# Two graph layers on one core: first loads in blocks, paired first projections, leading matmuls, adjacency waits by quarter

## The reference

```python
deg = sum(adj, -1)
agg = (adj @ x) / maximum(deg, 1e-6)
h = layernorm(x + relu(concat([x, agg], 2) @ W.T))
Ah = adj + eye(1024)
dh = rsqrt(sum(Ah, -1))
out = layernorm(h + relu((dh[:, :, None] * Ah * dh[:, None, :]) @ h @ K + bias))
```

## Time and profile before

| | |
|---|---|
| three runs | 513.21, 513.65, 514.17 us; median 513.65 |
| profiled execution | 514.48 us, of which the span is 512.3 us |
| TensorE | 494.2 us busy, 96% of the span, 3072 matmuls |
| VectorE | 388.8 us, 76% |
| ScalarE | 244.3 us, 48% |
| transfers | 59.78 MB, 117 GB/s over the span |

### The profile page before, as it was taken

One profiled execution on the slowest core, in us unless ns is written; L12 is line 12 of the kernel. 1 busy time (PEld: TensorE's weight loads), 2 busy tenths in 40 slices (PEclk: granted clock), 3 DMA queues, 4 the chain that ended last, 5 costly groups with the idle time before them and its releaser, 6 DMA issues.

```text
span 512.3 us, 8698 instructions
## 1 busy us (share of the span) xinstructions
PE 494.2 (96%) x3072; PEld 446.1 (87%) x3072; DVE 388.8 (76%) x1020; ACT 244.3 (48%) x483; POOL 0.7 (0%) x6
## 2 busy tenths in 40 slices
PE   4999999999999999999999999999999999999992
PEld 3899889988899888998889988998889988899872
DVE  4788487984889847987679858798397984898656
ACT  5735436374283542635444553636437364263312
POOL 0000000000000000000000000000000000000000
PEclk9999999999999999999999999999999999999997
DMA  8944401644018240372305531064401614020002
GB/s 280 377 153 166 157 8 41 210 159 164 0 56 278 75 164 0 104 265 67 137 0 174 223 119 58 0 246 164 164 0 41 246 41 164 0 83 1 0 1 82
DMA packets 15978, 59.78 MB, mean 117 GB/s; under 512 B 1760, under 2 KB 1888, under 8 KB 15072
## 3 DMA queue, kind: packets, MB, share of 16 engines
q1 hardware_dynamic: 15968, 59.64, 32.7%
HBM read 51.25 MB, written 8.39 MB: 116 GB/s over the span
## 4 chain that ended last, share of the span: by engine, by line
PE 96%; DVE 2%; DMA 1%; ACT 0%; SPq 0%; issue 0%; ACTq 0%
PE ring_a L586 24%; PE ring_a L590 12%; PE ring_b L602 11%; PE ring_b L603 11%; PE ring_b L604 11%; PE ring_b L562 6%; PE ring_b L564 6%; PE ring_b L563 6%; PE ring_a L562 3%; PE ring_a L563 3%; PE ring_a L564 3%; DMA x<-w 1%; DVE u L405 0%; DVE stats L414 0%; DVE x L409 0%
## 5 line engine op out<-in xcount | busy, mean ns | idle before, releaser
L586 PE MATMUL ring_a<-z_hi,adj_lo 128*128 128x258 f32 x512 | 103.2, 283 | 0.0
L586 PE MATMUL ring_a<-z_hi,adj_hi 128*128 128x258 f32 x512 | 102.5, 282 | 0.0
L590 PE MATMUL ring_a<-z_lo,adj_hi 128*128 128x256 f32 x512 | 101.3, 279 | 0.0
L602 PE MATMUL ring_b<-adj_hi,x1s_hi 128*128 128x512 f32 x256 | 99.9, 390 | 0.0
L603 PE MATMUL ring_b<-adj_lo,x1s_hi 128*128 128x512 f32 x256 | 99.7, 389 | 0.0
L604 PE MATMUL ring_b<-adj_hi,x1s_lo 128*128 128x512 f32 x256 | 99.7, 389 | 0.0
L586 PEld LDWEIGHTS ring_a<-z_hi,adj_lo 128*128 128x128 f32 x512 | 79.2, 189 | 0.0
L590 PEld LDWEIGHTS ring_a<-z_lo,adj_hi 128*128 128x128 f32 x512 | 79.0, 189 | 0.0
L586 PEld LDWEIGHTS ring_a<-z_hi,adj_hi 128*128 128x128 f32 x512 | 78.1, 188 | 0.1
L346 DVE TENSOR_TENSOR adj_lo<-adj_raw,adj_hi 128x1024 fp32r<-128x1024 f32 x64 | 75.0, 1221 | 3.8 <-ACT adj_hi L223 3.2
L223 ACT ACTIVATE adj_hi<-adj_raw 128x1024 fp32r<-128x1024 f32 x64 | 62.7, 1055 | 0.0
(11 more groups left out here) (66 smaller groups left out, 685.4 us busy)
## 6 DMA issues: line engine op xcount, KB each, us to landing
adj_raw<-adjT SPq DMA_DIRECT2D x64, 512.0 KB, 6.1
x_sb<-x SPq DMA_DIRECT2D x16, 512.0 KB, 4.9
out<-x SPq DMA_DIRECT2D x16, 512.0 KB, 2.6
xt_raw<-xT SPq DMA_DIRECT2D x7, 1024.0 KB, 4.8
x<-w SPq DMA_DIRECT2D x2, 256.0 KB, 4.0
xt_raw<-xT SPq DMA_DIRECT2D x2, 256.0 KB, 4.8
xt_raw<-xT SPq DMA_DIRECT2D x1, 512.0 KB, 6.2
x<-k SPq DMA_DIRECT2D x1, 256.0 KB, 8.9
```

Source lines behind the costliest of these rows:

```text
L586: nc.tensor.matmul(ring_a[:, t % NB + o, 0:F + 2], adj_block(a, h, j, i0 + o * P, P), z_hi[:, j, :], start=(j == 0 and a is a_hi), stop=False)
L590: last = nc.tensor.matmul(ring_a[:, t % NB + o, 0:F], adj_block(a_hi, h, j, i0 + o * P, P), z_lo[:, j, :], start=False, stop=(j == T - 1))
L602: nc.tensor.matmul(ring_b[:, bank, :], lhi, ahi, start=(j == 0), stop=False)
```

## The change

The layout of xT in DRAM and in SBUF becomes tile by tile (tile, f, column) instead of f by f, and xT arrives in pieces of two tiles with both f in them; w is stored as two whole blocks. The order of the first loads is w for f = 0, tiles 0 and 1, w for f = 1, tiles 2 and 3, tiles 4 to 7. The adjacency of half 1 is issued before the wait on `xt_lo_done` and before xT of batch 1. In later batches the rounding of xT is cut by tiles (0 to 3, 4 to 7) instead of by f, with the same sizes.

TensorE starts with 14 matmuls of 256 columns on a tile of ones (`x1s_hi`, filled by a memset at the head of VectorE's block), whose result is not used. Then tiles 0 and 1 are projected side by side in two banks, each kind of product as soon as its own operands are there: high by high needs no low part. The first adjacency blocks are split after every second projection instead of after each of the first four, and TensorE waits for them one by one, two source tiles at a time. TensorE's matmuls are the same otherwise. The unused semaphore names and the shapes of the buffers follow the layout.

```diff
@@ SP, the first loads
-            for f in range(FT):
-                sp.dma_start(w_raw[:, f, :], w[:, f, :]).then_inc(w_loaded[f], 16)
-                sp.dma_start(xt_raw[:, f, 0:NH], xT[0, :, f, 0:NH]).then_inc(xt0_loaded[f], 16)
-            sp.dma_start(xt_raw[:, :, NH:N], xT[0, :, :, NH:N]).then_inc(xt0_loaded[FT], 16)
+            pieces = ((0, 1), (1, 2), (2, XP))
+            for i, (first, end) in enumerate(pieces):
+                if i < FT:
+                    sp.dma_start(w_raw[:, i, :], w[i]).then_inc(w_loaded[i], 16)
+                sp.dma_start(xt_target(first, end), xt_source(0, first, end)).then_inc(xt0_loaded[i], 16)
             load_adj(0, 0)
             sp.dma_start(k_raw, k).then_inc(k_loaded, 16)
             sp.dma_start(bias_sb[:], bias).then_inc(bias_loaded, 16)
             load_x(0, 0)
+            load_adj(0, 1)
             sp.wait_ge(xt_lo_done, FT)
-            sp.dma_start(xt_raw[:], xT[1]).then_inc(xt_loaded, 16)
-            load_adj(0, 1)
+            sp.dma_start(xt_target(0, XP), xt_source(1, 0, XP)).then_inc(xt_loaded, 16)
             load_x(0, 1)
@@ ACT, the start (DVE follows the same order)
-            for f in range(FT):
-                act.wait_ge(w_loaded[f], 16)
-                copy(w_hi[:, f, :], w_raw[:, f, :]).then_inc(start_hi_done, 1)
-                act.wait_ge(xt0_loaded[f], 16)
-                copy(xt_hi[:, f, 0:NH], xt_raw[:, f, 0:NH]).then_inc(start_hi_done, 1)
-            act.wait_ge(xt0_loaded[FT], 16)
-            copy(xt_hi[:, :, NH:N], xt_raw[:, :, NH:N]).then_inc(xt_hi_done, FT)
+            act.wait_ge(w_loaded[0], 16)
+            copy(w_hi[:, 0, :], w_raw[:, 0, :]).then_inc(start_hi_done, 1)
+            act.wait_ge(xt0_loaded[0], 16)
+            copy(xt_pieces(xt_hi, 0, 1), xt_pieces(xt_raw, 0, 1)).then_inc(start_hi_done, 1)
+            act.wait_ge(w_loaded[1], 16)
+            copy(w_hi[:, 1, :], w_raw[:, 1, :]).then_inc(start_hi_done, 1)
+            for i, (first, end) in enumerate(((1, 2), (2, XP))):
+                act.wait_ge(xt0_loaded[i + 1], 16)
+                copy(xt_pieces(xt_hi, first, end), xt_pieces(xt_raw, first, end)).then_inc(xt_hi_done, 1)
             for t in range(T):
                 read_proj0(0, t, t % NB)
-                if t < CH:
-                    split_adj(0, 0, chunks=[t])
+                if t % 2 == 1:
+                    split_adj(0, 0, chunks=[t // 2])
@@ DVE
+            nc.vector.memset(x1s_hi[:, 0, :].bitcast(F32), 1.0).then_inc(warm_ready, 1)
@@ PE
+            def project0_first():
+
+                pe.wait_ge(warm_ready, 1)
+                for _ in range(WARM):
+                    nc.tensor.matmul(ring_a[:, 0, 0:F], x1s_hi[:, 0, 0:P], x1s_hi[:, 0, :],
+                                     start=True, stop=True)
                 for f in range(FT):
+                    pe.wait_ge(start_hi_done, 2 + f)
+                    for t in range(2):
+                        nc.tensor.matmul(ring_b[:, t, :], xt_hi[:, t, f, :], w_hi[:, f, :],
+                                         start=(f == 0), stop=False)
+                    pe.wait_ge(start_lo_done, 1 + 2 * f)
+                    for t in range(2):
+                        nc.tensor.matmul(ring_b[:, t, :], xt_hi[:, t, f, :], w_lo[:, f, :],
+                                         start=False, stop=False)
+                    pe.wait_ge(start_lo_done, 2 + f)
+                    for t in range(2):
+                        last = nc.tensor.matmul(ring_b[:, t, :], xt_lo[:, t, f, :], w_hi[:, f, :],
+                                                start=False, stop=(f == FT - 1))
...
             def aggregate_pair(b, t):
...
                     if t == 0:
+                        if j % JC == 0:
+                            pe.wait_ge(adj_lo_done, b * H * CH + j // JC + 1)
                         pe.wait_ge(z_lo_done, b * T + j + 1)
...
-                    if t % TH == 0:
-                        pe.wait_ge(adj_lo_done, b * H * CH + CH * (t // TH + 1))
+                    if t == TH:
+                        pe.wait_ge(adj_lo_done, b * H * CH + 2 * CH)
...
-            for t in range(T):
-                if t == TH:
-                    pe.wait_ge(xt_lo_done, FT)
+            project0_first()
+            for t in range(2, T):
+                if t == 2 or t == TH:
+                    pe.wait_ge(xt_lo_done, t // 2)
@@ DRAM layout (the inputs are laid out before the launch)
-        "xT": x.reshape(B, N, FT, P).transpose(0, 3, 2, 1),
-        "w": w.reshape(F, 2, FT, P).transpose(3, 2, 1, 0).reshape(P, FT, 2 * F),
+        "xT": x.reshape(B, XP, T // XP, P, FT, P).transpose(0, 1, 5, 2, 4, 3).reshape(B, XP, P, T // XP * FT * P),
+        "w": w.reshape(F, 2, FT, P).transpose(2, 3, 1, 0).reshape(FT, P, 2 * F),
```

More of the change, by code:

```diff
@@ L20 @@
 PL = 6
+XP = 4
+WARM = 14
 DEG_EPS = 1e-6
@@ L48, in gnn_two_layers @@
         diag = sb("adj_diag", [P, T, P])
-        xt_raw = sb("xt_raw", [P, FT, N])
-        xt_hi = sb("xt_hi", [P, FT, N], F32R)
-        xt_lo = sb("xt_lo", [P, FT, N], F32R)
+        xt_raw = sb("xt_raw", [P, T, FT, P])
+        xt_hi = sb("xt_hi", [P, T, FT, P], F32R)
+        xt_lo = sb("xt_lo", [P, T, FT, P], F32R)
         g1_hi = sb("g1_hi", [P, FT, NH], F32R)
@@ L96, in gnn_two_layers @@
         k_loaded, bias_loaded = sem("k_loaded"), sem("bias_loaded")
-        xt0_loaded = [sem(f"xt0_loaded{i}") for i in range(FT + 1)]
+        xt0_loaded = [sem(f"xt0_loaded{i}") for i in range(3)]
         xt_loaded = sem("xt_loaded")
@@ L102, in gnn_two_layers @@
         x1_free = [sem(f"x1_free{h}") for h in range(H)]
+        warm_ready = sem("warm_ready")
         ident_zero, ident_done, ones_done = sem("ident_zero"), sem("ident_done"), sem("ones_done")
@@ L133, in gnn_two_layers, with xt_pieces, xt_source, xt_target @@
         block = ctx.enter_context(nc.Block())
+        def xt_pieces(t, first, end):
+            return t[:, first * T // XP:end * T // XP, :, :].rearrange("p t f c -> p (t f c)")
+        def xt_source(n, first, end):
+            return xT[n, first:end].rearrange("q p m -> p q m")
+        def xt_target(first, end):
+            return xt_pieces(xt_raw, first, end).rearrange("p (q m) -> p q m", q=end - first)
         def adj_block(t, h, j, i0, n):
@@ L153, in g_part @@
             if h == 0:
-                return (xt_hi if hi else xt_lo)[:, f, 0:NH]
+                first = (xt_hi if hi else xt_lo)[:, 0:TH, :, :].rearrange("p t f c -> p (t f c)")
+                return first[:, f * NH:(f + 1) * NH]
             return (g1_hi if hi else g1_lo)[:, f, :]
@@ L234, in split_xt @@
                 act.wait_ge(xt_loaded, 16 * n)
-                for f in range(FT):
-                    copy(xt_hi[:, f, :], xt_raw[:, f, :]).then_inc(xt_hi_done, 1)
+                for i in range(FT):
+                    copy(xt_pieces(xt_hi, 2 * i, 2 * i + 2),
+                         xt_pieces(xt_raw, 2 * i, 2 * i + 2)).then_inc(xt_hi_done, 1)
             def read_proj0(n, t, bank):
@@ L360, in split_xt @@
             def split_xt(n):
-                for f in range(FT):
-                    dve.wait_ge(xt_hi_done, n * FT + f + 1)
-                    minus(xt_lo[:, f, :], xt_raw[:, f, :], xt_hi[:, f, :]).then_inc(xt_lo_done, 1)
+                for i in range(FT):
+                    dve.wait_ge(xt_hi_done, n * FT + i + 1)
+                    minus(xt_pieces(xt_lo, 2 * i, 2 * i + 2), xt_pieces(xt_raw, 2 * i, 2 * i + 2),
+                          xt_pieces(xt_hi, 2 * i, 2 * i + 2)).then_inc(xt_lo_done, 1)
             def read_proj0(n, t, bank):
@@ L531, in _ @@
             nc.vector.tensor_copy(z_hi[:, :, F:F + 2], ones[:]).then_inc(z_ones_done, 1)
[L532 to L538, removed]
+            dve.wait_ge(start_hi_done, 1)
+            minus(w_lo[:, 0, :], w_raw[:, 0, :], w_hi[:, 0, :]).then_inc(start_lo_done, 1)
+            dve.wait_ge(start_hi_done, 2)
+            minus(xt_pieces(xt_lo, 0, 1), xt_pieces(xt_raw, 0, 1),
+                  xt_pieces(xt_hi, 0, 1)).then_inc(start_lo_done, 1)
+            dve.wait_ge(start_hi_done, 3)
+            minus(w_lo[:, 1, :], w_raw[:, 1, :], w_hi[:, 1, :]).then_inc(start_lo_done, 1)
+            for i, (first, end) in enumerate(((1, 2), (2, XP))):
+                dve.wait_ge(xt_hi_done, i + 1)
+                minus(xt_pieces(xt_lo, first, end), xt_pieces(xt_raw, first, end),
+                      xt_pieces(xt_hi, first, end)).then_inc(xt_lo_done, 1)
             for t in range(T):
                 read_proj0(0, t, t % NB)
-                if t < CH:
-                    split_adj(0, 0, t, t + 1)
+                if t % 2 == 1:
+                    split_adj(0, 0, t // 2, t // 2 + 1)
             dve.wait_ge(ident_done, 1)
@@ L567, in project0 @@
             def project0(n, t, bank):
-                cols = slice(t * P, (t + 1) * P)
-                for f in range(FT):
[L571 to L576, removed]
+                product(ring_b[:, bank, :],
```

(9 more changed lines are left out.)

3 lines of the change are left out of this document (1 added, 2 removed).

## The result

| | before | changed |
|---|---|---|
| runs | 513.21, 513.65, 513.67, 514.17 | 509.07, 509.56, 509.72, 509.75 |
| median | 513.66 us | 509.64 us |
| profiled execution, span | 514.48, 512.3 | 509.72, 507.5 |

The ratio is 0.9915, with a 95% interval of 0.9903 to 0.9928: 4.0 us by the medians, 3.7 to 5.0 by the interval, where 2.3 was forecast. It is faster, by nearly twice as much as the sum said; the median lies just inside the range of 509.3 to 512.9, near the value of rival A (509.6). One later run of the kernel before, of 2816 us, is a slow one and is left out of every comparison.

What follows compares the result with a forecast made beforehand. TensorE's matmuls bound the kernel, so only the time before the first aggregation could change. Clock and earlier start 2.24 us plus loads 0.1 gave 2.3 us, 513.65 to 511.3 us; range 509.3 to 512.9.

Steps and rivals of the forecast that it cites:

- rival A: Start: leading matmuls raise the clock before 6.05 us and it stays up; 4.1 us gained, 509.6; chance 0.17.
- part 1: Start, order and pairs: first real matmul at 6.05 us, both later waits go, unbroken run begins 2.92 us earlier.
- Part 5: Splits and waits: fourth adjacency block ready 3.1 us after first aggregation starts, hidden by quarter waits; cost 0.
- Part 4: Loads and blocks: gapless blocks land between 0.3 us later and 0.5 us earlier; 0.1 us earlier taken.
- Part 2: Clock at the start: rises 5.26 us into the unbroken run, first aggregation 19.55; gain 2.24 us, bounds 0.9 to 4.1.
- Part 3: The 14 leading matmuls before the real work: end by 4.4 us, cost nothing on the path, counted at nothing.
- B: Start: clock's rise is not tied to the unbroken run, stays near 14.2 us; 0.9 us gained, 512.75; chance 0.13.
- C: Behind the first aggregation: DVE's backlog becomes TensorE's wait at t = 4; 1.1 us slower, 514.8; chance 0.03.
- D: Start: leading matmuls run to 8.6 us, projections start late at the high clock; 2.2 us gained, 511.4; chance 0.05.

Runs made afterwards that it cites:

- the one wait: The changed kernel, but TensorE waits for all four low adjacency blocks before the first aggregation; 514.69 us, ratio 1.0014.
- rest in two: The changed kernel with the last load of xT (tiles 4 to 7) in two parts, projections 0 and 1 read between them; 509.55 us, ratio 0.9930.

## Why the prediction fell short

**What held.** The bound was read rightly: only the time before the first aggregation moved. It lies between 16.3 and 21.8 us in the profiles, and 490.4 or 490.5 us lie behind it in all of them but two, those of the old load order (491.2) and of the one wait (492.1, with the half clock in it). The pairs take away both waits of the start (part 1), as the variant without the blocks shows; in the changed kernel, with its earlier start, two short ones come in their place (w_lo at 7.21, the bank at 11.50). Part 5's cost of nothing held too: the fourth adjacency block was ready at 18.92 + 1.23 = 20.15, that is 3.07 us after the first aggregation (3.1 forecast), add_layer0 started 8.7 us after it (8.9 forecast), and TensorE waited for neither.

**Part 4 is the step that failed most.** "I take 0.1 us earlier", from bounds of 0.3 us later to 0.5 earlier; the blocks brought the first part of xT at least 1.1 us sooner (4.23 against 5.36), and taking them away costs 2.2 us. My upper bound came from the rates of the windows in the earlier trace rows, 310 against 409 GB/s, and the 310 was no rate of this load: that window opens at 5.40, when the first part of xT is there. In the stretches in which it travelled the rate was 229 and 263 GB/s, against 309 and 282 in the changed kernel. Its own time from issue to ACT's start, 5.36 - 1.20 = 4.2 us, has become at most 4.23 - 1.19 = 3.0.

**Part 2's 5.26 us was one draw.** Counted as there, from the last wait to the rise, the time was 2.9 us without leading matmuls, 3.1 without the pairs, 3.6 and 4.7 in the kernel before with only the leading matmuls or only the blocks, and 4.1 to 4.2 with 7 leading matmuls and without the blocks. The Trainium skill (TensorE: Matmul & The Clock Gate, Part 1: The HAM clock gate) says that the number of slow matmuls varies from run to run with the same kernel. The runs here fit that, though each profile is of a variant of its own: in five of them the start is the same, with 14 leading matmuls and pauses of 0.30 to 0.60 us, and the clock was up at the first real matmul in two, and 1 to 2 us later in the other three. In the profiles the real work started 1.1 us sooner than forecast (4.91 against 6.05) and the first aggregation came 2.5 sooner (17.08 against 19.55). The other 1.3 us are the clock: twelve slow matmuls were forecast (2.4 us) and none is there, less 1.1 us of waits for data. Without leading matmuls only six were slow, and the first aggregation was at 17.30.

I had also set the difference of one profiled execution against the median of others: the one of before, at 514.48, was above every run then shown. A first aggregation at 19.55 means 19.55 + 490.5 + 2.2 = 512.2 us, and not 511.3, so this step hid 0.9 us of the miss.

**Part 3 was short too.** "I count them at nothing"; they are worth 0.7 us in the changed kernel (510.35 without). The reason I gave, that a pause undoes them, fits the runs: nothing with a pause of 2.2 us, nothing with 7 and a pause of 1.8. What I left out is that the parts act on each other. With the load at least 1.1 us earlier the pause is 0.36 us and not 1.5.

**The rivals.** A (17.7 us, 509.6) has the number, and the profiled execution has its early clock; but that the time is near its value is in good part luck. A counts on a start at 6.05 and on the leading matmuls for all that it adds, and without them the kernel still takes only 510.35. B, C and D did not happen; C is seen in small where the old load order was put back.

**The parts.** Each taken from the changed kernel alone costs: the blocks 2.2 us, the pairs 1.35, the leading matmuls 0.7, the late splits 0.35 and the load order 0.2 (both within the scatter). Taking out the waits by quarter costs 5.0 while the splits are late. Added to the kernel before, the leading matmuls bring nothing and the blocks some 0.3 to 0.5. The parts do not add up; they shorten the same stretch together.

## What to carry to other kernels

Where a start waits for a load, look at the landing of that one transfer and at its layout in DRAM, and take a rate only from the stretch in which it travels; here gapless blocks of 256 KB gave 1.1 us or more. Leading matmuls paid here only where they ended within 0.4 us or so of the real work without holding it up: 14 gave 0.7 us, 7 nothing, and 28 nothing either. In the kernel before, whose real work starts later, 28 gave 2.0 us and 14 nothing. So tune their number together with the landing, and again when the landing moves. A stall of TensorE of 3 us cost more than its length in seven of ten runs: count the half clock behind it too, and cut one wait for all of an operand into waits for its parts.

## What the runs showed that I had not expected

Where the clock rose near the start, by profile. All times are from TensorE's timeline, and each row is a single execution. In the kernel before, the real work itself has a gap before the second f, of 0.55 to 0.75 us (1.20 behind the 28).

| leading matmuls | pause before the real work | high clock from, counted from the first real matmul |
|---|---|---|
| 14, changed kernel | 0.36 us | the first real matmul |
| 14, old load order | 0.60 | the first real matmul |
| 14, old splits | 0.36 | 1 us after it |
| 14, one wait; 14, rest in two | 0.30; 0.32 | 2 us after it |
| 14, no pairs | 1.00 | 3 us after it |
| 7 | 1.82 | 4 us after it |
| 14, no blocks | 2.06 | 4 us after it |
| 14, kernel before | 2.21 | 6 us after it, 3.6 after the gap |
| 28, changed kernel; 28, kernel before | 0.0 | within the leading ones |
| none, changed kernel | - | 3 us after it |
| none, kernel before with the blocks | - | 7 us after it, 4.7 after the gap |
| none, kernel before | - | 7.5 us after it, 5.3 after the gap |

A leading run of matmuls that ended 2 us early left the time no better than none (513.67 against 513.4 in the kernel before, 510.39 against 510.35 in the changed one). And a higher clock from the start was worth little by itself: in the changed kernel 1.1 us of it went back into waits for data (4.91, the start-up of 0.1 and 48 matmuls at the high clock would give 16.0, with 17.08 measured), so that the variant without leading matmuls reached its first aggregation only 0.2 us later in its profile. Where the clock was up at the first real matmul with the old load order, the 14 leading ones took 3.19 us instead of 3.35, so it rose at their very end.
